# A state-space layer and a mixture of experts on one core: dbu made for four states at a time, products with C two at a time, new orders

## The reference

```python
xz = x @ W_in + b_in                       # to 2 x 256
x_proj, z = jnp.split(xz, 2, axis=-1)
x_conv = silu(x_proj)
A = -jnp.exp(A_log)                        # 256 x 16
B, C = jnp.split(x_conv @ W_xproj + b_xproj, 2, axis=-1)     # 16 states each
dt = jax.nn.softplus(x_conv @ W_dt + b_dt)
# per token t: h = h * exp(dt*A) + (dt*u) B ;  y = sum_s h C + D u
y = selective_scan(x_conv, dt, A, B, C, D_param) * silu(z)
x = x + y @ W_out + b_out
```

```python
scores = softmax(xt @ gate_w.T);  _, indices = top_k(scores + gate_bias, 2)
y = sum_e mlp(xt, w1[e], w2[e], w3[e]) * combine[:, e];  out = x + y + mlp(xt, sw1, sw2, sw3)
```

## Time and profile before

| | us |
|---|---|
| three runs | 1292.01, 1288.14, 1292.46; median 1292.01 |
| the profiled execution | 1290.66 |
| its span, first to last instruction | 1288.5 |

### The profile page before, as it was taken

The page is one execution under the profiler, slowest core; times in us unless marked ns, Lnnn a source line. Parts: engine busy times, 40 slices in busy tenths (PEclk is TensorE's granted clock), DMA queues, the critical chain, the costliest instruction groups (busy, mean ns, idle before and its releaser), DMA issues.

```text
span 1288.5 us, 25674 instructions
## 1 busy us (share of the span) xinstructions
PE 1179.8 (92%) x7200; PEld 946.2 (73%) x7200; DVE 1174.2 (91%) x1833; ACT 1126.6 (87%) x1965; POOL 1112.8 (86%) x902
## 2 busy tenths in 40 slices
PE   4565899999999999999999999999999999999998
PEld 2334587877878787787778777777878778788887
DVE  1779899999999999999999999999999999999954
ACT  6674889999998999999899999989989998999854
POOL 2999899898999989899998989999898999998700
PEclk8776899999999999999999999999999999999999
DMA  8233331605234160523415052331505243250000
GB/s 305 121 146 125 133 148 39 250 1 207 82 132 155 54 232 0 205 81 137 150 62 225 0 205 81 144 142 67 220 0 210 77 152 135 71 208 9 10 9 9
DMA packets 47942, 152.74 MB, mean 119 GB/s; under 512 B 4512, under 2 KB 29472, under 8 KB 31392
## 3 DMA queue, kind: packets, MB, share of 16 engines
q1 hardware_dynamic: 47904, 152.28, 31.3%
HBM read 147.03 MB, written 5.24 MB: 118 GB/s over the span
## 4 chain that ended last, share of the span: by engine, by line
POOL 27%; issue 23%; PE 22%; DVE 19%; ACT 7%; DVEq 1%; DMA 0%; POOLq 0%; ACTq 0%; SPq 0%
POOL dbu L673 16%; PE h L938 10%; POOL hc L681 7%; DVE da L773 6%; PE mixed L907 5%; DVE hc L773 5%; PE y_acc L920 4%; POOL dt_s L661 3%; DVE g L815 2%; ACT L625 2%; ACT silu L625 2%; ACT da L589 1%; DVE acc L823 1%; DVE stats L743 1%; DVE hc L781 1%
## 5 line engine op out<-in xcount | busy, mean ns | idle before, releaser
L673 POOL TENSOR_TENSOR dbu<-w_s,b_all 128x512 f32<-128x512 f32 x512 | 650.3, 1289 | 5.7 <-DVE da L773 3.0
L681 POOL TENSOR_TENSOR hc<-hc,c_all 128x512 f32<-128x512 f32 x272 | 350.5, 1292 | 82.1 <-DVE hc L773 80.6
L589 ACT ACTIVATE da<-dt_s,a_neg 128x512 f32<-128x512 f32 x512 | 346.7, 692 | 84.2 <-DVE hc L781 70.0
L773 DVE TENSOR_TENSOR_SCAN hc<-da,dbu 128x512 f32<-128x512 f32 x272 | 328.1, 1211 | 12.0 <-PE y_acc L920 10.9
L920 PE MATMUL y_acc<-ident,hc 128*128 128x128 f32 x2048 | 295.0, 280 | 32.5 <-POOL hc L681 27.3
L773 DVE TENSOR_TENSOR_SCAN da<-da,dbu 128x512 f32<-128x512 f32 x240 | 292.6, 1219 | 27.4 <-ACT da L589 15.1
L920 PEld LDWEIGHTS y_acc<-ident,hc 128*128 128x128 f32 x2048 | 247.5, 144 | 81.5 <-POOL hc L681 36.2
L907 PE MATMUL mixed<-w_s,g 128*128 128x128 f32 x2304 | 283.4, 276 | 3.2 <-DVE g L815 1.2
L907 PEld LDWEIGHTS mixed<-w_s,g 128*128 128x128 f32 x2304 | 270.6, 192 | 15.4 <-DVE g L815 10.1
L938 PE MATMUL h<-x_hi,w_hi 128*128 128x512 f32 x576 | 264.1, 458 | 7.4 <-DVE g L815 2.9
L938 PE MATMUL h<-x_hi,w_lo 128*128 128x512 f32 x576 | 228.4, 396 | 0.0
(11 more groups left out here) (77 smaller groups left out, 1063.6 us busy)
## 6 DMA issues: line engine op xcount, KB each, us to landing
b_all<-bc_rows SPq DMA_DIRECT2D x64, 1024.0 KB, 4.7
c_all<-bc_rows SPq DMA_DIRECT2D x64, 1024.0 KB, 6.8
xt<-in_x SPq DMA_DIRECT2D x16, 256.0 KB, 6.5
res<-in_x SPq DMA_DIRECT2D x16, 256.0 KB, 6.9
out<-acc SPq DMA_DIRECT2D x16, 256.0 KB, 2.3
silu<-in_w SPq DMA_DIRECT2D x6, 256.0 KB, 4.1
w_s<-in_w SPq DMA_DIRECT2D x1, 1152.0 KB, 6.9
bc_rows<-bc_rows_s SPq DMA_DIRECT2D x16, 64.0 KB, 1.6
```

The costliest lines, as they stand in the source:

```text
L589: act.activation(da[a % DA_SLOTS][:, :], dt_s[:, c, :], ACT.Exp, scale=a_neg[:, a:a + 1]).then_inc(decay_made, 1)
L673: pool.tensor_tensor(dbu[:, a % DBU_SLOTS, :], w_s[:, c, :], b_all[:, s, :], ALU.mult).then_inc(dbu_made, 1)
L681: pool.tensor_tensor(slot, slot, c_all[:, s, :], ALU.mult).then_inc(c_by_pool, 1)
L773: dve.tensor_tensor_scan(dst, ring[:, :], dbu[:, a % DBU_SLOTS, :], 0.0, ALU.mult, ALU.add).then_inc(scanned, 1)
```

## The change

- `DBU_SLOTS` 8, `AT_ONCE = 4`: one dbu makes four states, 128x2048, into one half of the ring; it waits for the last scan of the quarter that was there. A scan waits for the dbu of its quarter.
- `BY_DVE` are the steps 0, 1 of every four (16 in all, 15 before), `BY_POOL` 2 and 3; hcp works on both of a pair, 128x1024, after the second scan.
- The additions of eps go from VectorE (agg) to GpSimd (rs).
- In rank, the scores and a second copy of the biased scores lie in PSUM, in the bank of route, and the bank is freed by rank.7 and not rank.6.
- `ORDER`, `START_ORDER` and `END_ORDER` are new. START_ORDER now writes out windows 0 to 2, END_ORDER 14, 15 and what follows; the loop runs from 4 to 13 (window 3 is written out before it). A window now holds the scans of the sequence before and the experts of three before; a sequence's experts still start late in the scans of the next sequence.

```diff
-DA_SLOTS, DBU_SLOTS, HC_SLOTS = 2, 4, 4
+DA_SLOTS, DBU_SLOTS, HC_SLOTS = 2, 8, 4
+AT_ONCE = 4
+DBUS = STEPS // AT_ONCE
-BY_DVE = [0, 2, 4, 6, 8, 10, 12, 14, 16, 18, 20, 22, 24, 26, 28]
+BY_DVE = [0, 1, 4, 5, 8, 9, 12, 13, 16, 17, 20, 21, 24, 25, 28, 29]
...
 ORDER, "dve":
-        scan.14 mul.14 scan.15 nb2.0-1 g.14-2 scan.16 scan.17 mul.16 comb.6-2 scan.18 g.15-2 mul.18 scan.19
+        mul.16-1 scan.17-1 g.11-3 mul.17-1 scan.18-1 scan.19-1 g.12-3 scan.20-1 g.13-3 g.14-3 scan.21-1
...
                 if what == "rs1":
+                    wait_apart(pool, moments1_made, m + 1)
+                    pool.tensor_scalar(var_eps[:, :], moments[:, :, 1], EPS, None, ALU.add).then_inc(var1_made, 1)
                     pool.wait_ge(var1_made, m + 1)
...
                 elif what == "dbu":
-                    c, s = a // NS, a % NS
+                    step = AT_ONCE * a
+                    c, s = step // NS, step % NS
...
-                    wait(pool, scanned, STEPS * m + a + 1 - DBU_SLOTS)
-                    pool.tensor_tensor(dbu[:, a % DBU_SLOTS, :], w_s[:, c, :], b_all[:, s, :],
-                                       ALU.mult).then_inc(dbu_made, 1)
+                    user, back = before(step + AT_ONCE - 1, DBU_SLOTS, STEPS)
+                    if not (isinstance(m, int) and m == 0 and back):
+                        pool.wait_ge(scanned, STEPS * (m - back) + user + 1)
+                    at = step % DBU_SLOTS
+                    pool.tensor_tensor(dbu[:, at:at + AT_ONCE, :], w_s[:, c, None, :].broadcast_to([P, AT_ONCE, T]),
+                                       b_all[:, s:s + AT_ONCE, :], ALU.mult).then_inc(dbu_made, 1)
                 elif what == "hcp":
-                    pool.wait_ge(scanned, STEPS * m + a + 1)
+                    pool.wait_ge(scanned, STEPS * m + a + 2)
...
+                    pair = hc[:, at:at + 2, :]
+                    pool.tensor_tensor(pair, pair, c_all[:, s:s + 2, :], ALU.mult).then_inc(c_by_pool, 1)
...
-            def rank_step(i, m, tile, ranked):
-                other = biased[:, :, None, :].broadcast_to([P, NB, E, E])
+            def rank_step(i, m, tile):
+                at = E * E + NB * E * E
+                score, other = (tile[:, at + i * NB * E:at + (i + 1) * NB * E].rearrange("p (b e) -> p b e", b=NB)
+                                 for i in range(2))
...
                 elif i == 3:
-                    step = dve.tensor_tensor(biased[:, :, :], score[:, :, :],
-                                             gb_s[:, None, :].broadcast_to([P, NB, E]), ALU.add)
+                    for dst in (biased[:, :, :], other):
+                        step = dve.tensor_tensor(dst, score, gb_s[:, None, :].broadcast_to([P, NB, E]), ALU.add)
                 elif i == 4:
-                    step = dve.tensor_tensor(ahead, other, own, ALU.subtract)
+                    step = dve.tensor_tensor(ahead, other[:, :, None, :].broadcast_to([P, NB, E, E]), own, ALU.subtract)
...
                     for b in range(NB):
                         last = dve.bn_aggr(mom[:, b, :], st[:, b, :])
                     last.then_inc(done, 1)
-                    dve.wait_ge(done, m + 1)
-                    dve.tensor_scalar(var[:, :], mom[:, :, 1], EPS, None, ALU.add).then_inc(ready, 1)
...
-                    dve.wait_ge(dbu_made, STEPS * m + a + 1)
+                    dve.wait_ge(dbu_made, DBUS * m + a // AT_ONCE + 1)
```

More of the change, by code:

```diff
@@ L118 @@
+        spread.1+1 spread.2+1 spread.3+1 load.0+3 rows.0+2 spread.0+2 spread.1+2
     """,
@@ L202, in __init__, with place_in_window @@
         self.place = {task: i for i, task in enumerate(self.order)}
+    def place_in_window(self, name, a, off):
+        here, full = self.offset[name, a], len(self.window)
+        first = self.place[name, a, LAG + here] + (off - here - LAG) * full
+        assert all(self.place[name, a, n + off] == first + n * full for n in LOOP)
+        return first
     def use(self, name, a, n, off):
@@ L217, in bank @@
             return use % self.banks, use // self.banks
-        first = self.place[name, a, LAG + self.offset[name, a]] + (off - self.offset[name, a] - LAG) * len(self.window)
+        first = self.place_in_window(name, a, off)
         return first % self.banks, n * (len(self.window) // self.banks) + first // self.banks
@@ L226, in user_before @@
         at = self.window.index((name, a, off)) - self.banks
-        name, a, off = self.window[at]
-        return name, a, n + off - (1 if at < 0 else 0)
+        user, b, there = self.window[at]
+        there -= 1 if at < 0 else 0
+        assert all(self.order[self.place[name, a, k + off] - self.banks] == (user, b, k + there)
+                   for k in LOOP)
+        return user, b, n + there
 MIXED_TURN = InTurn(MIXED, MIXED_BANKS)
```

281 lines of the change are left out of this document (175 added, 106 removed).

## The result

| | us |
|---|---|
| four runs of the changed kernel | 1256.58, 1255.87, 1260.27, 1256.79; median 1256.68 |
| the kernel before beside them | median of four runs 1291.03 |
| ratio, with its 95% interval | 0.9742 (0.9716 to 0.9768) |
| span of the profiled execution | 1254.8 (before 1288.5) |

The change makes the kernel 2.6% faster. The forecast was 1273, with a range of 1254 to 1295: the direction and the range held, and the size of the gain was too small by 16 us, 34 measured against 18.5.

A forecast was written before the change was run, and what follows sets the result against it. VectorE was read as nearest to the 74.82 us period, with ScalarE late next at 73.2. Start 162, eleven windows 805.2, end part 236.7 and tail 66.1 gave 1270.0 us of span, 1272.2 in time (1273 on the median); range 1254 to 1295.

The forecast's parts named there:

- The waits of the coarse grain: GpSimd's product and long dbu released together by a quarter's last scan; costed at nothing in the loop.
- 1.6 + 0.6: ScalarE's idle us per loop window: 1.6 ahead of silu and scaling, 0.6 for the rest, on 71.0 busy.
- The first rival: All engines keep up with VectorE in the loop: period 72.65 us, time 1258; chance 0.17.
- The start: Up to the scan of state 29 of sequence 1: near 162 us against 167.4, bounds 157 and 186.
- The splits' term: Nine w_lo splits in the start: 12 us more on VectorE, 4 on the path; GpSimd held 5.5 us.
- GpSimd's chain: GpSimd's dbu and products in the start, back to back, bring sequence 1's dbu.7 to 150.1 us.
- The rival of no saving per state: One dbu over four states saves nothing per state: 8 us at the start, time 1281; chance 0.09.
- The unchanged period: Loop period stays at 74.8 us, TensorE or ScalarE idling as before; time 1290, chance 0.13.
- ScalarE as a bound at 76.15: ScalarE keeps 5.15 us idle beside 71.0 busy per loop window; period 76.15, time 1311, chance 0.09.
- the splits at a whole dbu each: In the start each w_lo split waits out a whole dbu: start 186 us, time 1296; chance 0.04.
- The tail: The stretch behind the last window, with no scan left: 66.1 us against 63.0.
- The end part: Between the loop windows and the tail, set by TensorE's time: 236.7 us.

The follow-up runs named there:

- e9: The kernel before with eps additions on GpSimd, scores also written to PSUM and both biased copies made from there; 1273.73 us.
- e12: The changed kernel with eps additions on VectorE, rank 4 reading SBUF twice, and each dbu as four 512-column instructions; 1280.75 us.
- e1: The changed kernel with the nine w_lo splits freed of their second SBUF input, by a second ScalarE copy into a bank of h; 1246.29 us.
- e4: The changed kernel with both inputs of rank 4's subtraction read from SBUF again; 1321.55 us.
- e5: The kernel before with eps additions on GpSimd and rank 4 reading a PSUM copy of the biased scores, scores staying in SBUF; 1278.75 us.
- e2: The changed kernel with each dbu as four instructions of 512 columns in place of one of 2048; 1255.84 us.
- e11: The changed kernel with the splits freed as in e1 and each dbu as four instructions of 512 columns; 1250.78 us.

## Why the prediction was right, and where it was off

**The mechanism of the loop** was right in its parts. Rank 4 was put at 0.43 us and took 0.42; the last step of rank 0.19 and 0.18; a dbu 4.65 and 4.58; a product of two 2.4 and 2.38; one more table load a window, 14 (56 + 40 + 8 + 8 over eight windows); the products' idle time gone; GpSimd with slack. The waits of the coarse grain cost nothing in the loop, as was said.

**The step that failed is ScalarE's idle time**, the term "1.6 + 0.6". The prediction took what stood ahead of silu and the scaling as TensorE's, which "stays". Measured is 0.26 us ahead of silu and none ahead of the scaling, 0.9 us in all against the 2.2 of the forecast. TensorE was the releaser, but TensorE itself was waiting. Two groups of TensorE of the kernel before, over the windows of the earlier trace rows, which the prediction did not use:

```profile
L881 PE MATMUL mixed<-xnT,win_s 128*128 128x512 f32 x64 | 31.5, 615 | 9.6 <-DVE acc L823 9.6
...
L845 PE MATMUL mixed<-ident,y_s 128*128 128x128 f32 x64 | 10.0, 279 | 8.4 <-DVE rank L713 8.4
```

18.0 us over eight windows, 2.25 a window, behind VectorE's additions of the experts and behind rank. The changed kernel has none of it. e9 shows that VectorE's relief alone takes the wait ahead of silu away, and e12 that the new order alone does it too; the scaling's wait stays in e9 and goes with the new order. The period is 71.2 us and not 73.2. Of the 2.0 us between them 1.3 are this idle time, and 0.7 are ScalarE's busy time, 70.3 where the forecast had 71.0. The added table load came (10.2 us over eight windows); the decays' group is 2.8 us shorter over the eight windows and silu's 1.7 longer, and where the rest of the 0.7 went the groups don't show. The same error made TensorE's 71.9 us look like a floor. It was not one: TensorE's busy time fell to 70.8 a window with the same matmuls, whose mean durations hardly changed (y_acc 273 and 273 ns, eo 276 and 277), so the 71.9 held some time that was not work. Matmul ends are modelled in the profile, and no run tests what that time was.

**The first rival**, all engines keep up with VectorE, came nearest, 1258 us. It was given 0.17 and its own period of 72.65 was too long as well: VectorE's busy time fell by 2.8 us a window (581.4 to 559.3 over eight), where the terms gave 1.8, and its idle time by 0.85 where they gave 0.4. Of the missing busy time the groups show 0.6 us in the scans (310.3 to 305.4 us for 256) and 0.2 in the added product, 82.7 to 85.9 us over eight windows.

**The start** came 7.8 us later than forecast. The splits' term was right in size: 23.7 us were reckoned for nine (11.7 + 12), 25.0 measured, and on the path 4 + 5.5 against the 10.0 that e1 takes away. How the 10.0 divide between VectorE's waits and GpSimd held up, which were priced apart, no run shows. GpSimd's chain without them was right too, the last dbu forecast for 150.1 and in e1 at 152.05. What failed is the last sentence, "scans 28 and 29 end 2.3 us later": they end 7.7 us later in e1 and 5.7 in the changed kernel, where the last dbu ends at 164.1. There VectorE waits for slots of hc that TensorE frees late. In e1 TensorE works through that wait at a granted clock of 0.50, as shown above; the forecast has no term for TensorE in the start. The rule of the Trainium skill that the prediction cites for the splits ("SBUF — State Buffer", section "Who interferes with whom") is borne out in its direction by e1, e4 and e5. In its words the lock is held for a whole instruction; e2's split waited for the one that ran and six behind it, 9.1 us, so here "one instruction" is not an upper bound.

**The rival of no saving per state** was wrong in its sign: a long dbu saves 0.4 us on GpSimd (4.58 against four times 1.24), and e11 shows what all of them are worth, 4.5 us. But its time effect in the changed kernel is nothing (e2), because the splits wait longer behind it. The unchanged period, ScalarE as a bound at 76.15, and the splits at a whole dbu each did not come: three of the nine splits took 4.3 us or more, the first three 0.9 to 1.9.

**End part and tail.** The tail was right within 1 us, 66.1 against 65.6. The end part took 233.1 us and not 236.7. It was reckoned with TensorE's 71.9 us a window, and with the 70.8 of the changed kernel the same sum gives 233.2: it is the loop's error once more. The last three windows show TensorE busy 222.15 of 224.49 us, so it is the bound there, as was said.

**That the time fell into the range was luck.** The errors had opposite signs: 18.9 us of gain missed in the eleven windows and 3.6 in the end part, 7.8 us of loss missed in the start. The range was laid over periods of 72.65 to 74.8 us, and the measured 71.2 lies below both. With the start as forecast the time would have been near 1249 us, below the range.

Three smaller points of the prediction's text don't follow from what it shows. The chances of the first three cases add up to 0.74, so "faster" had at least that and not 0.71. The earlier trace rows put 1.7 of the 4.9 us of idle time ahead of the products behind the scan, which is not most of it, though nearly all of it went. The range takes 175 us as the upper bound of the start, where the start's own paragraph has 186.

## What to carry to other kernels

An idle time's releaser is only the last link: before "this wait stays" is written down, look at what the releasing engine waits for itself, since here TensorE's and ScalarE's waits went when VectorE was relieved, and went as well when the order was changed. Before GpSimd instructions are made longer, every VectorE instruction with two inputs in SBUF should get one of them from PSUM; in a loop its wait has one fixed phase, so a mean over phases is no price, and a bad case is nearly a whole long instruction in every round, and TensorE's clock can fall behind it. An addition of known size on each engine in turn shows what a percentage of busy time doesn't: an engine with 2% idle may have no reserve at all.
